# A state-space phase: the inverse transform in even and odd halves, two branches joined in the projection, and its output copied by ScalarE and added by GpSimd

## What is computed

```python
dA = jnp.exp(jnp.einsum('bdl,dn->lbdn', delta, A))
dBu = jnp.einsum('bdl,bnl,bdl->lbdn', delta, Bm, x)
def step(h, ab):
    h = ab[0] * h + ab[1]
    return (h, h)
_, hs = lax.scan(step, jnp.zeros_like(dA[0]), (dA, dBu))
y = jnp.einsum('lbdn,bnl->bdl', hs, Cm) + Dp[None, :, None] * x
return y * jax.nn.silu(z)
```

## Time and profile before

| what | value |
|---|---|
| time, median of 3 runs | 2165.59 us (2164.03 to 2168.28) |
| time of the profiled execution | 2169.39 us |
| its span, first to last instruction | 2167.6 us |
| busy: TensorE, VectorE, ScalarE, GpSimd | 2020.1, 1686.2, 1374.7, 1112.7 us |
| mean granted TensorE clock | 0.965 of full |

### The profile page before, as it was taken

One profiled execution on the slowest core, in us unless ns is written; L12 is line 12 of the kernel. 1 busy time (PEld: TensorE's weight loads), 2 busy tenths in 40 slices (PEclk: granted clock), 3 DMA queues, 4 the chain that ended last, 5 costly groups with the idle time before them and its releaser, 6 DMA issues. The chain is left out here.

```text
span 2167.6 us, 40610 instructions
## 1 busy us (share of the span) xinstructions
PE 2020.1 (93%) x14620; PEld 1506.8 (70%) x14620; DVE 1686.2 (78%) x2918; ACT 1374.7 (63%) x2687; POOL 1112.7 (51%) x1509
## 2 busy tenths in 40 slices
PE   6999999986999995999999988699999999999878
PEld 4677777754887773677777755577877877877745
DVE  5777777765888875777777765499999999999974
ACT  1677777763777773677777653467586685685633
POOL 3555555623767764555555512345736647556423
PEclk8899999997999997999999997899999999999989
DMA  4655566530000003555555515000000000000000
GB/s 133 148 149 147 146 148 149 145 106 1 2 2 2 2 2 78 151 149 146 149 145 150 150 31 200 1 1 1 1 1 1 1 1 0 1 0 1 1 15 20
DMA packets 147750, 144.94 MB, mean 67 GB/s; under 512 B 14048, under 2 KB 106976, under 8 KB 146912
## 3 DMA queue, kind: packets, MB, share of 16 engines
q1 hardware_dynamic: 127968, 132.91, 22.4%
q10 hardware_dynamic: 19584, 9.44, 2.4%
HBM read 94.07 MB, written 38.80 MB: 61 GB/s over the span
## 5 line engine op out<-in xcount | busy, mean ns | idle before, releaser
L606 DVE TENSOR_REDUCE sb_f_mx<-ps_f_s 128x2 f32<-128x512 f32 x768 | 506.4, 686 | 216.5 <-PE ps_f_s L354 215.6
L530 ACT ACTIVATE sb_f_pt<-ps_f_t 128x1024 f32<-128x1024 f32 x384 | 382.1, 1023 | 114.9 <-issue 56.2
L1954 POOL TENSOR_TENSOR sb_mb_h<-sb_mb_h 128x512 f32<-128x512 f32 x128 | 165.0, 1310 | 303.4 <-DVE sb_mb_h L1837 302.3
L354 PE MATMUL ps_f_s<-sb_f_stack 96*128 96x256 bf16 x1536 | 286.5, 279 | 22.1 <-DMA sb_f_stack<-f_scr 14.1
L1832 DVE TENSOR_TENSOR_SCAN sb_mb_h<-sb_mb_da,sb_mb_h 128x1024 f32<-128x1024 f32 x128 | 304.4, 2418 | 2.7 <-ACT sb_mb_da L1692 2.7
L1503 PE MATMUL ps_mb_f<-sb_mb_fc,sb_mb_cw 128*128 128x256 f32 x1280 | 286.8, 381 | 6.7 <-ACT sb_mb_fc L1705 6.6
L1503 PEld LDWEIGHTS ps_mb_f<-sb_mb_fc,sb_mb_cw 128*128 128x128 f32 x1280 | 239.7, 190 | 41.4 <-ACT sb_mb_fc L1705 8.9
L371 PE MATMUL ps_f_t<-sb_f_stack 128*128 128x256 bf16 x1536 | 232.9, 274 | 6.3 <-ACT sb_f_pt L530 3.3
L1692 ACT ACTIVATE sb_mb_da<-sb_mb_dl,sb_mb_an 128x255 f32<-128x255 f32 x512 | 211.0, 496 | 31.3 <-DVE sb_mb_h L1832 30.7
L354 PEld LDWEIGHTS ps_f_s<-sb_f_stack 96*128 96x128 bf16 x1536 | 140.7, 99 | 109.7 <-issue 41.3
L427 PE MATMUL ps_f_a<-sb_f_pt,sb_f_v 128*32 128x256 f32 x3072 | 188.8, 387 | 1.6 <-ACT sb_f_v L579 1.6
(11 more groups left out here) (252 smaller groups left out, 4132.7 us busy)
## 6 DMA issues: line engine op xcount, KB each, us to landing
f_scr<-sb_f_parts SPq DMA_DIRECT2D x96, 384.0 KB, 2.7
sb_f_stack<-f_scr SPq DMA_DIRECT2D x192, 192.0 KB, 3.0
sb_f_stack<-f_scr SPq DMA_DIRECT2D x192, 128.0 KB, 3.1
sb_f_stack<-f_scr SPq DMA_DIRECT2D x192, 64.0 KB, 3.3
sb_f_stack<-sb_f_mrow ACTq DMA_DIRECT2D x96, 96.0 KB
sb_mb_cw<-in_cw SPq DMA_DIRECT2D x1, 5120.0 KB, 19.4
sb_prep_wn<-in_wn SPq DMA_DIRECT2D x6, 512.0 KB, 7.7
sb_m_w<-in_w SPq DMA_DIRECT2D x6, 256.0 KB, 3.1
```

The costliest lines, as they stand in the source:

```text
L354: last = nc.tensor.matmul(s_bank[j % 2][:, h, :], stack[0:ROWS, a.n % STACKS, 0, g * GROUP + pair * 2 + h, half * P:(half + 1) * P], stack ...
L530: nc.scalar.activation(pt[:, e.two, g, half, :, :], t_bank[i % 2][:, :, :], ACT.Exp).then_inc(s["pt_sb"], 1)
L606: nc.vector.tensor_reduce(mx[:, a.two, half, head:head + 2], s_bank[j % 2][:, :, :], AX.X, ALU.max)\
L1954: nc.gpsimd.tensor_tensor(hb[:, c, 0:2, :], hb[:, c, 0:2, :], hb[:, c, 2:4, :], ALU.add).then_inc(s["half_sb"], 1)
```

## The change

- The inverse transform over channels (slot 6) computes the first 128 of each 256 columns only, from the even and the odd frequencies apart. The inputs are reordered for it on the host (`parity`), the convolution's output channels with them. ScalarE copies the four halves into `fc`, and GpSimd (`meet`) forms their sum and difference in `uk`.
- The join on VectorE goes; `project_out` accumulates both branches, with 8 matmuls in place of 4.
- The output is copied by ScalarE into `dts` in slot 7 (`oc_sb`) and added to `x` by GpSimd. The z projection waits for the copy.
- The energy goes to GpSimd, the magnitude (Abs) to ScalarE. Square root, scaling, statistics and normalization of o move by about a slot.
- ScalarE evacuates the inverse transform (`frequency(m, 6)`) ahead of `decay(m, 7)`.
- At the head: the first B spread and the combination of the gate weights move to slot 4 of the first step, `decay(m, 1)` of the first sequence ahead of the evacuation of the gate weights, the last transposes go into other banks.
- Attention and mixture of experts end with a square root of one element on ScalarE (`root_table`).

The core of the diff:

```diff
+    def root_table(self):
+        self.nc.scalar.activation(self.spare[:, :], self.eps[:, :], ACT.Sqrt)
...
@@ TensorE
                     pe.wait_ge(s["u_sb"], 2 * f.b + 2)
-                    since(pe, "x_sb", f.b - 1)
+                    since(pe, "oc_sb", f.b - 1)
...
-                elif slot == 6:
-                    kc = half
-                    if kc == 0:
-                        pe.wait_ge(s["f_sb"], seen + 4)
-                    for c in range(XC_CH):
-                        last = nc.tensor.matmul(f_bank[(1 + kc) % 2][:, :], fs[:, c, kc * P:(kc + 1) * P], gi[:, c, :],
-                                                start=c == 0, stop=c == XC_CH - 1)
...
+                elif slot == 6 and half == 0:
+                    pe.wait_ge(s["f_sb"], seen + 4)
+                    for kc in range(2):
+                        for odd in range(2):
+                            for ri in range(2):
+                                c = 2 * ri + odd
+                                last = nc.tensor.matmul(f_bank[kc][:, odd * N:(odd + 1) * N], fs[:, c, kc::2],
+                                                        gi[:, c, :].rearrange("p (t a n) -> p t a n", t=2, a=2)[:, :, 0, :],
+                                                        start=ri == 0, stop=ri == 1)
+                    last.then_inc(s["f_ps"], 1)
                 elif slot == 7 and half == 1:
-                    pe.wait_ge(s["f_sb"], seen + 5)
+                    pe.wait_ge(s["uk_sb"], m.b + 1)
...
-                    for c in range(DC):
-                        last = nc.tensor.matmul(w_bank[:, 0, half * P:(half + 1) * P], ys[:, o.parity, c, half * P:(half + 1) * P],
-                                                wop[:, c, :], start=c == 0, stop=c == DC - 1)
+                    for n, t in enumerate((ys[:, o.parity, :, :], vv)):
+                        for c in range(DC):
+                            last = nc.tensor.matmul(w_bank[:, 0, half * P:(half + 1) * P], t[:, c, half * P:(half + 1) * P],
+                                                    wop[:, c, :], start=n + c == 0, stop=n + c == DC)
...
                     if m and slot == 6:
                         total(m, slot - 2)
                         direct(m, 0)
+                        direct(m, 1)
                         spread(m, slot, 1)
...
-                    if m and slot == 7:
-                        direct(m, 1)
...
+                    if f and f.b == 0 and slot == 4:
+                        combine()
+                        spread(f, 0, 0)
@@ ScalarE
                 if m and m.b == 0:
                     front(m, 7)
+                    decay(m, 1)
                     act.wait_ge(s["gw_ps"], 1)
...
-                if o:
-                    act.wait_ge(s["sq2_sb"], o.b + 1)
-                    nc.scalar.activation(vv[:, :, :], vv[:, :, :], ACT.Sqrt).then_inc(s["v_sb"], 1)
...
-                    if m and slot < UNITS - 1:
+                    if m and slot == 6:
+                        frequency(m, slot)
+                    if m and slot < UNITS - 1 and (m.b or slot):
                         decay(m, slot + 1)
-                    if m and 1 < slot < UNITS - 1:
+                    if m and 1 < slot < 6:
                         frequency(m, slot)
-                    if o and slot == 0:
+                    if o and slot == 1:
+                        act.wait_ge(s["sq2_sb"], o.b + 1)
+                        nc.scalar.activation(vv[:, :, :], vv[:, :, :], ACT.Sqrt).then_inc(s["v_sb"], 1)
+                        act.wait_ge(s["zmax"], o.b + 1)
+                        nc.scalar.activation(zo[:, :], zm[:, :], ACT.Abs).then_inc(s["zo_sb"], 1)
...
                     if f and f.b and slot == 6:
                         softplus(f, slice(0, 2))
+                    if o and slot == 7:
+                        act.wait_ge(s["o_ps"], o.b + 1)
+                        nc.scalar.activation(dts[:, :], w_bank[:, 0, :], ACT.Copy).then_inc(s["oc_sb"], 1)
                     if f and f.b and slot == 7:
                         front(f, 7)
@@ VectorE: energy, join and add_output go; zo without its magnitude
@@ GpSimd
+            def meet(m):
+                pool.wait_ge(s["f_sb"], m.b * FREQ + 5)
+                v = uk[:, :, :].rearrange("p k (t a n) -> p k t a n", t=2, a=2)
+                eo = fc[:, :, PAD:PAD + N].rearrange("p (k e) (t n) -> p k e t n", k=2, t=2)
+                nc.gpsimd.tensor_tensor(v[:, :, :, 0, :], eo[:, :, 0, :, :], eo[:, :, 1, :, :], ALU.add)
+                nc.gpsimd.tensor_tensor(v[:, :, :, 1, :], eo[:, :, 0, :, :], eo[:, :, 1, :, :], ALU.subtract).then_inc(s["uk_sb"], 1)
+            def energy(o):
+                pool.wait_ge(s["f_sb"], FREQ * (o.b + 1))
+                since(pool, "o_ps", o.b)
+                nc.gpsimd.tensor_tensor(vv[:, :, :], sq[:, :, 0:N], sq[:, :, N:2 * N], ALU.add).then_inc(s["sq2_sb"], 1)
+            def add_output(o):
+                pool.wait_ge(s["oc_sb"], o.b + 1)
+                xs = k.x[:, 2 * o.b:2 * o.b + 2, :].rearrange("p t e -> p (t e)")
+                nc.gpsimd.tensor_tensor(xs, xs, dts[:, :], ALU.add).then_inc(s["x_sb"], 1)
...
             def step(f, m, o):
+                if o:
+                    energy(o)
                 for un in range(UNITS):
+                    if m and un == UNITS - 2:
+                        meet(m)
                     if f and un in BC_SLOTS:
                         parts(f, BC_SLOTS.index(un))
+                    if o and un == OUT_SLOT + 1:
+                        add_output(o)
                     if m:
                         halve(m, un)
```

More of the change, by code:

```diff
@@ L1404, in mamba_phase @@
         ny = k.sb("mb_ny", [P, B, 2, D], ctx)
[L1405 removed]
+        norm = Front(k, "mb", ctx, [t.rearrange("p a n -> p (a n)") for t in (b_bank[:, 0:2, :], c_bank[:, 0:2, :], c_bank[:, 2:4, :], y_bank[:, :, :])], ny)
         names = ["stx_sb", "zeroed", "consts", "wc_sb", "an_exp", "sel_sb", "xb_sb",
@@ L1531, in spread @@
                 if un == 0 and m.b == 0:
-                    pe.wait_ge(norm.xT_sb, B // 2)
+                    pe.wait_ge(norm.xT_sb, B // 2 if which else 1)
                     pe.wait_ge(s["sel_sb"], 1)
-                if un == 0:
+                    pe.wait_ge(s["bc_sb"], 1)
+                elif un in (0, SU):
                     pe.wait_ge(s["bc_sb"], 2 * m.b + 2)
@@ L1588, in step @@
             def step(f, m, o):
-                if m and m.b == 0:
-                    combine()
                 for slot in range(UNITS):
-                    if o and slot < 2:
+                    if o and slot < 2 and not m:
                         total(o, UNITS - 2 + slot)
@@ L1606, in step @@
                         frequency(m, slot, 1)
+                    if o and m and slot == 0:
+                        total(o, UNITS - 2)
                     if f and slot in (1, 7):
                         project(f, slot)
+                    if o and m and slot == 1:
+                        total(o, UNITS - 1)
                     if m and slot not in (0, 6):
@@ L1623, in step @@
                         frequency(m, slot, 1)
-                    if f and slot == UNITS - 1:
+                    if f and f.b and slot == UNITS - 1:
                         spread(f, 0, 0)
@@ L1649, in front @@
                     nc.scalar.activation(bcf[:, :], w_bank[:, 0, :], ACT.Copy).then_inc(s["bcf_sb"], 1)
+                    if r == 0:
+                        since(act, "x_sb", f.b - 2)
                     nc.scalar.activation(dts[:, :], w_bank[:, 1, :], ACT.Copy).then_inc(s["dts_sb"], 1)
@@ L1658, in front @@
                     act.wait_ge(s["z_ps"], f.b + 1)
-                    since(act, "yt_sb", f.b - 1)
+                    since(act, "ym_sb", f.b - 1)
+                    since(act, "zmax", f.b - 1)
                     nc.scalar.activation(sz[:, f.parity, :, :], w_bank[:, :, :], ACT.Silu).then_inc(s["sz_sb"], 1)
@@ L1702, in frequency @@
                 elif slot == 1:
+                    since(act, "uk_sb", m.b)
                     for part in range(2):
@@ L1716, in frequency @@
                     for kc in range(2):
-                        last = nc.scalar.activation(uk[:, kc, :], f_bank[(1 + kc) % 2][:, :], ACT.Copy)
+                        last = nc.scalar.activation(fc[:, 2 * kc:2 * kc + 2, PAD:PAD + N],
+                                                    f_bank[kc][:, :].rearrange("p (c n) -> p c n", c=2), ACT.Copy)
                     last.then_inc(s["f_sb"], 1)
@@ L1751, in step @@
                         last.then_inc(s["vz_sb"], 1)
-                    if o and slot == 2:
+                    if o and slot == 3:
                         act.wait_ge(s["mv_sb"], DC * (o.b + 1))
                         nc.scalar.activation(sd[:, :], mv[:, :, 1], ACT.Sqrt, bias=k.eps[:, :]).then_inc(s["sd_sb"], 1)
-                    if o and slot == 3:
+                    if o and slot == 4:
                         act.wait_ge(s["nm_sb"], o.b + 1)
```

(25 more changed lines are left out.)

26 lines of the change are left out of this document (8 added, 18 removed).

## The result

The changed kernel takes **2203.71 us** (median, 2202.87 to 2207.01) against 2165.32 for the kernel before (2164.03 to 2168.28): a ratio of **1.0181, interval 1.0169 to 1.0194**. It is slower by 38 us; the prediction said 28, with a range that holds the time. The profiled execution has a span of 2201.1 us, 33.5 more than before.

The account below looks back on a forecast made before the run. Full TensorE and VectorE, under 2 us slack each, make semaphore waits decisive. Six held steps +29.2, loads -2.6, head -1, ends +2.4 give +28 us: 2193.6 us from the median, range 2178 to 2206.

Parts of the forecast that it names:

- z held by ScalarE's order: Slot 7, six full steps: TensorE stands 7.8 us at z, waiting for ScalarE's late output copy; chance 0.76.
- ScalarE's chain: From transform's end to output copy: start, two evacuations, table loads, decays, softplus, copy; 10.8 us.
- TensorE's work: Full step: 84.77 less waits and shorter transform, plus extra projection products; 80.5 us.
- Step without clock loss: Full step closed through ScalarE's copy, then z, C spread and last transform: 88.2 us.
- the rival with 2214 us: Inverse transform: strided weight loads at half rate, 3.45 us more in each of six steps; chance 0.06.
- VectorE idle 8 us or more per step: Sign expected in the changed profile's timeline if z is held: VectorE idles at least 8 us per step.
- The clock loss: TensorE behind the stop at z: lowered clock costs 1.4 us per step, bounds 0 and 1.7.
- Head and first step: Start of state-space phase: gate weights behind decays, combination earlier, shorter transform; -1 us, from -4 to +3.
- The loads: Two table loads ahead of phases' first roots move into the phase before: -2.6 us, bounds -2.6 and 0.
- The ends: Last two steps and tail: VectorE's relief gains 2.1 us, the tail costs 4.5; together +2.4 us.
- The rival "faster": Full steps: z is not held, step 81.5 us, total 2145 us; chance 0.14.
- the second one: Full steps: no hold at z, but GpSimd's new work slows VectorE's scans; 84.6 us, total 2163.5; chance 0.04.

Follow-up runs that it names:

- the filled run: Changed kernel with 8 extra unused 128x512 matmuls on TensorE ahead of each held z projection: 2190.5 us, ratio 1.0116.
- the filled runs: Changed kernel with 16 or 8 extra unused matmuls on TensorE ahead of each held z projection: 2226.82 us and 2190.5 us.
- the vector add: Changed kernel with VectorE adding the projected output from PSUM in slot 6, without ScalarE's copy and GpSimd's add: 2166.41 us, ratio 0.9993.
- the combined version: Changed kernel with VectorE's output add, decays and gate weights first; last sequence: energy on VectorE, first output products ahead of the wait: 2153.42 us.

## Why the prediction was right, and where it was off

**The mechanism** was right in every link of the held step. z held by ScalarE's order: 7.58 us for 7.8. ScalarE's chain: 10.8 for 10.8, with 1.29 us from each of its two table loads to the activation behind it, as the prediction took from its row. TensorE's work: 80.5 for 80.5. Step without clock loss: 88.2 for the 88.34 that the filled run shows (its stop and filling are the old stop). The transform with strided weights: 16 records in 3.46 us, as for contiguous ones, so the rival with 2214 us is out. VectorE idle 8 us or more per step: 9.7. Four runs that freed z or shortened its stop, each in another way, took 27 to 37 us off.

**The clock loss was mis-sized.** This is the term that failed most. The prediction took 1.4 us from two late waits, with 1.7 as the bound. By comparing with the filled runs it is 2.2 (90.52 - 88.34) to 2.4 (90.52 - 94.25 + 13.73 - 7.58), by the records 1.7 to 3.0. The rows it was taken from are one transform over channels and one part of the convolution, behind waits of 0.2 and 2.7 us, each read once. Behind the stop at z the loss runs over three rows (z, C spread, transform) and varies from step to step at an equal stop, so one reading of one row was no bound. In six steps this is 5 to 6 of the 10 us by which the sum fell short of the measured 38.

**Head and first step,** taken as -1 with a range to +3, were the second term. Up to the second z the phase gained 1.8 us on the kernel before, but to the third z it lost 9.4, 4.5 more than a full step's forecast. Behind the second z TensorE waits 1.16 us for GpSimd's meeting of the halves and 2.41 for VectorE, and what follows is slow again (L1490 takes 3.19 us, in the later steps 1.96):

```profile
1481.28 7.13 PE L1530 MATMUL ps_mb_f<-sb_mb_gi,sb_mb_uk 128*128 128x512 f32 x16 [1.16 <-POOL sb_mb_uk L1966]
...
1491.26 1.01 PE L1547 MATMUL ps_mb_c<-sb_mb_bc,sb_mb_sel 128*128 128x256 bf16 x4 [2.41 <-DVE sb_mb_h L1865]
1492.07 3.19 PE L1490 MATMUL ps_mb_f<-sb_mb_fa,sb_mb_ny 128*128 128x512 f32 x4
```

The prediction had said that GpSimd's work costs nothing because TensorE stands at z; in this first step there is no copy to stand for, and so no such cover. The part up to the second z would have been a gain of 7.8 without the gate weights' wait, by the run that undid it; the range had priced the decays ahead of them (4.6 us), not the slow clock behind the wait (3.78 us for 1.98). In the time, undoing it gives 4.3 us.

**The loads,** -2.6: none that the runs can tell from zero, the other end of the range given. **The ends,** +2.4: from the end of the last held transform to the last measure it is 93.65 us for 93.55, so +0.1, and the +2.9 from the last z are the sixth step's slow clock. The last phase adds +1.1, which the prediction didn't have. The order in the tail is as worked out, with the energy behind the halving on GpSimd; the size of its +4.5 and of the 2.1 set against it was not tested singly:

```profile
2116.66 1.40 POOL L1958 TENSOR_TENSOR sb_mb_h<-sb_mb_h 128x256 f32<-128x256 f32 x2
2118.02 1.26 POOL L1972 TENSOR_TENSOR sb_mb_vv<-sb_mb_uk 128x512 f32<-128x512 f32 x1
```

**The rival "faster" had a wrong price.** It said 2145 us for a z that isn't held. Two kernels in which it isn't held take 2166.5. Its step of 81.5 assumed VectorE at 80.2 and a microsecond of handover; measured are 83.8 and 83.9. The nearer rival for that case was the second one, GpSimd giving it back, with 84.6 and 2163.5: the prediction had written that GpSimd's work is hidden by the stop and loses that cover if the stop goes, and had then not put that cost into the price of the case where it goes. So where the expected gain of the change went has two answers. As written, into the stop at z. With the stop away, TensorE's 2.5 us and VectorE's 4.6 us per step still buy under 1 us (84.8 to 83.9): VectorE is at 97%, with instructions that take 1.1 us more per step beside GpSimd, and each of the two engines waits about 2 us per step (with the vector add, TensorE 2.1 for VectorE at the C spread, VectorE 1.1 for the output projection and 0.8 for decays). That is read from the traces; only the combined version tests part of it, and gets one more microsecond per step.

## What to carry to other kernels

An engine that frees a buffer late in its program order is a wait for whoever writes the buffer next: before moving a copy to another engine, list what stands ahead of it there and compare its end with the moment the next writer arrives. In TensorE's order, put the product that needs the freed bank behind work that doesn't: here that alone gave back 37 us. And when a stop hides another engine's new work, price the two together, since mending the stop uncovers it.

## What the runs showed of the hardware that was not expected

- A short stop can cost TensorE as much clock as a long one, but not each time. Lost by z, C spread and transform (8.17 us at full speed), in six steps each: behind 3.0 us of idling 1.6 to 3.1 us, 2.2 on average; behind 3.3 us 0.1 to 3.1, 1.6 on average; behind 7.6 us 1.7 to 3.0, 2.35 on average.
- Work that nobody needs made the kernel faster: 16 records of 0.43 us in the stop, and 13 us less in the whole.
- A 512-column fp32 product leaves two records of 0.43 us at full clock, so 16 products took 13.7 us; count records, not calls.
- GpSimd beside a scan: 2.65 us for 0.67, 3.36 for 1.29, 6.34 for 2.50, while the pair of scans beside the last went from 4.46 to 5.60.
